# Graph network kernel: convolutions that read a 16-bit copy of the edge counts, with features in three 16-bit parts

## What is computed

```python
def gcn_conv(x, W, b, src, dst, n_nodes):
    ones = jnp.ones(src.shape[0], dtype=x.dtype)
    deg = jax.ops.segment_sum(ones, dst, num_segments=n_nodes)
    dinv = jnp.where(deg > 0, jax.lax.rsqrt(deg), 0.0)
    norm = dinv[src] * dinv[dst]
    h = x @ W
    msg = h[src] * norm[:, None]
    out = jax.ops.segment_sum(msg, dst, num_segments=n_nodes)
    return out + b
...
h = gcn_conv(x, W1, b1, src, dst, n)
h = jax.nn.relu(h)
h = gcn_conv(h, W2, b2, src, dst, n)
return jax.nn.log_softmax(h, axis=1)
```

## Time and profile before

| | us |
|---|---|
| median of 3 runs | 3497.33 (3475.69 to 3510.03) |
| the profiled execution | 3489.9 |
| its span, first to last instruction | 3488.1 |
| PE busy, of the span | 2740.4 (79%) |
| DVE busy | 2218.7 (64%) |
| ACT busy | 1601.9 (46%) |
| DMA, mean over the span | 117 GB/s |

### The profile page before, as it was taken

How to read it: one execution, slowest core, us unless ns; L and a number is a source line. 1 busy time by engine, 2 the same in 40 slices (tenths; PEclk the granted TensorE clock), 3 DMA queues, 4 the chain that set the end, 5 groups by cost and what they waited for, 6 DMA issues and landing times. The chain is left out here.

```text
span 3488.1 us, 63284 instructions
## 1 busy us (share of the span) xinstructions
PE 2740.4 (79%) x21694; PEld 2254.5 (65%) x21694; DVE 2218.7 (64%) x4911; ACT 1601.9 (46%) x2729; POOL 201.0 (6%) x481
## 2 busy tenths in 40 slices
PE   2887777524354888798883999979998999979998
PEld 1555554402043666576662898969897899968997
DVE  8999998300046999799995555555555555545555
ACT  1555554200023888688883444434444444434443
POOL 1000000000000000000000111001110111001110
PEclk9999999767657999889996999999999999989999
DMA  2666666795805333532320333223331233223331
GB/s 56 149 148 148 148 149 163 166 238 143 196 2 160 113 113 113 157 113 102 111 91 9 133 112 127 94 78 112 126 110 71 103 125 110 94 76 118 121 112 54
DMA packets 164745, 406.93 MB, mean 117 GB/s; under 512 B 123705, under 2 KB 135793, under 8 KB 136048
## 3 DMA queue, kind: packets, MB, share of 16 engines
q1 hardware_dynamic: 164573, 404.67, 39.7%
HBM read 322.84 MB, written 80.77 MB: 116 GB/s over the span
## 5 line engine op out<-in xcount | busy, mean ns | idle before, releaser
L1604 DVE CUSTOM_DVE_ANT_0 l_arow<-l_scores,abias 125x500 f32<-125x500 f32 (+1 forms) x525 | 325.5, 622 | 368.6 <-issue 314.7
L1540 PE MATMUL l_asum<-vals,l_awcol 125*125 125x129 f32 x3750 | 516.2, 277 | 34.6 <-DVE l_awcol L934 34.3
L1540 PEld LDWEIGHTS l_asum<-vals,l_awcol 125*125 125x125 f32 x3750 | 454.6, 187 | 61.9 <-DVE l_awcol L934 52.9
L1193 PE MATMUL gturned<-ident,grow 125*125 125x125 f32 x2500 | 410.3, 306 | 30.0 <-ACT grow L1133 30.0
L1193 PEld LDWEIGHTS gturned<-ident,grow 125*125 125x125 f32 x2500 | 333.0, 204 | 108.0 <-issue 73.2
L1102 DVE SCALAR_TENSOR_TENSOR grow<-line,a_dst 125x3125 f32<-125x3125 f32 x100 | 347.6, 3476 | 52.4 <-DMA line<-lines_dram 44.1
L1575 ACT ACTIVATE l_arow<-l_arow,l_aneg 125x500 f32<-125x500 f32 (+1 forms) x525 | 323.5, 659 | 81.1 <-DVE l_aneg L1610 81.1
L932 ACT ACTIVATE l_awcol<-l_aturned 125x500 f32<-125x500 f32 (+1 forms) x225 | 122.8, 546 | 516.2 <-PE l_aturned L1549 516.2
L1133 ACT ACTIVATE grow<-grow,neg 125x3125 f32<-125x3125 f32 x100 | 290.4, 2904 | 137.3 <-DVE neg L1114 137.3
L1111 DVE CUSTOM_DVE_ANT_0 grow<-grow,bias 125x3125 f32<-125x3125 f32 x100 | 341.7, 3417 | 16.8 <-DMA bias<-bias_dram 1.8
L1171 PE MATMUL gparts<-gwcol,h_mem 125*32 125x125 f32 x5000 | 244.5, 291 | 122.2 <-ACT gwcol L1146 122.2
(11 more groups left out here) (300 smaller groups left out, 4464.4 us busy)
## 6 DMA issues: line engine op xcount, KB each, us to landing
abias<-bias_dram SPq DMA_DIRECT2D x100, 1562.5 KB, 6.5
bias<-bias_dram SPq DMA_DIRECT2D x50, 1562.5 KB, 6.5
counts<-counts_dram SPq DMA_DIRECT2D x41, 1367.2 KB
bias_dram<-lnrow SPq DMA_DIRECT2D x25, 1562.5 KB, 6.8
counts_dram<-blk SPq DMA_DIRECT2D x25, 1367.2 KB
line<-lines_dram SPq DMA_DIRECT2D x8, 1367.2 KB
counts<-counts_dram SPq DMA_DIRECT2D x41, 158.7 KB
fixed<-kp SPq DMA_DIRECT2D x250, 4.0 KB, 2.5
```

Source lines behind the costliest of these rows:

```text
L1193: last = pe.transpose(bank[q % RING][:, j // 4, j % 4 * T:(j % 4 + 1) * T], row[n % RING][:, t * T:(t + 1) * T], ident[0:T, 0:T])
L1540: last = pe.matmul(sum_ps[p][:, :], wcol[c % T_BANKS][:, j * T:(j + 1) * T], vals[:, t, :], start=(t == 0), stop=(t == NT - 1))
L1604: dve.tensor_tensor_reduce(out=row[p][:, a:z], in0=s_ps[c % S_BANKS][:, 0:z - a], in1=bias[p][0:T, a:z], scale=1.0, scalar=-3.0e38, op0=AL ...
```

## The change

The counts are also written as bf16, to a second array `counts16_dram` (0.78 MB a tile). In `build_counts` ACT casts five rows of `blk` in each slot (125 casts of 125 x 625 elements), and SP writes two blocks of destinations at a time (runs of 500 bytes, as before), in slot 2 of every odd block from b = 3 on, eleven times while blocks are still being made, once in the last step and once, for the single last block (runs of 250 bytes), after the last `bias_home`. The fp32 counts are still written.

In the convolution stage, `u` is split by DVE into three bf16 parts (`in_pieces`), which stand side by side in 48 of 64 columns (`u_pieces`). PE takes the tiles in pairs on 64 columns each, thirteen groups a round, in bf16. Fourteen tiles are loaded in the first block, 20 are held. Counts over 256 are not exact in bf16, so a loop after the fourth group of each round reads whole fp32 tiles into `agg`, takes off the rounded part, and adds the product of the rest in fp32. It runs once where no degree is over 256, and 25 times otherwise; the trip count comes from the largest degree, found in the first block (`most`, `trips`). ACT's copies of the sums now start chunk by chunk (`sum_ready`), and so does PE's turn.

```diff
+        blk16 = [sb(f"blk16_{p}", [T, NT, 2 * T], BF16) for p in range(2)]
...
+                def counts16_home(q):
+                    blocks = range(2 * q, min(2 * q + 2, NT))
+                    sp.wait_ge(cast_done, SLOTS * (blocks[-1] + 1))
+                    a, z = blocks[0] * T, (blocks[-1] + 1) * T
+                    load_rows(sp, G["counts16_dram"][:, :, a:z].rearrange("t s d -> s t d"), blk16[q % 2][:, :, 0:z - a], counts16_out[q % 2])
...
                         counts_home(b - 1)
                     if k == 1 and b >= 2:
                         bias_home(b - 2)
+                    if k == 2 and b >= 3 and b % 2 == 1:
+                        counts16_home((b - 3) // 2)
                 bias_home(NT - 1)
+                counts16_home(NT // 2)
...
+                            act.wait_ge(cast_done, SLOTS * (b - 1))
                             act.wait_ge(counts_out[b % 2], LANDED * (b // 2))
...
+                        q, half = g // 2, g % 2
+                        if k == 0:
+                            act.wait_ge(win_read, 2 * SLOTS * b)
+                            if half == 0 and q >= 2:
+                                act.wait_ge(counts16_out[q % 2], LANDED * (q // 2))
+                        part = slice(NT // SLOTS * k, NT // SLOTS * (k + 1))
+                        act.activation(blk16[q % 2][:, part, half * T:(half + 1) * T], blk[g % 2][:, part, :], ACT.Copy).then_inc(cast_done, 1)
...
-    SLOTS, EARLY = 9, 6
+    EARLY, LATE, PIECES, WIDE_U = 14, 2, 3, 64
+    SLOTS = (EARLY + 4 + LATE) // 2
+    EXACT = 256
...
-        for r, order in enumerate((range(NT), [*range(NT - SLOTS, NT), *range(NT - SLOTS)])):
-            for i, t in enumerate(order):
-                if i % 4 == 0:
-                    groups.append([])
-                if t not in held:
+        for order in (range(len(pairs)), [*range(len(pairs) - SLOTS, len(pairs)), *range(len(pairs) - SLOTS)]):
+            for i in order:
+                if i not in held:
                     slot = len(loads) if len(loads) < SLOTS else held.pop(next(iter(held)))
-                    loads.append((t, slot, last_use[slot]))
-                    held[t] = slot
-                last_use[held[t]] = len(groups)
-                groups[-1].append((t, held[t], sum(1 for _, k, _ in loads if k == held[t])))
+                    loads.append((i, slot, last_use[slot]))
+                    held[i] = slot
+                groups.append((i, held[i], sum(LANDED * len(pairs[k]) for k, there, _ in loads if there == held[i])))
+                last_use[held[i]] = len(groups)
+        final = [[max(g for g, (i, _, _) in enumerate(groups) if g // half_groups == r and len(pairs[i]) > j) for j in range(2)] for r in range(2)]
+        def load(sp, n):
+            i, slot, after = loads[n]
             if after:
                 sp.wait_ge(group_used, after)
-            load_rows(sp, counts[slot][:, :], G["counts_dram"][t, :, :], counts_in[slot])
+            for j, t in enumerate(pairs[i]):
+                load_rows(sp, counts[2 * slot + j], G["counts16_dram"][t, :, :], counts_in[slot])
+        def in_pieces(dve, m, rest):
+            piece = lambda k: u_pieces[:, :, k * HID:(k + 1) * HID]
+            chain(dve, m, dve.tensor_copy(piece(0), u[:, :, :]))
+            chain(dve, m, dve.tensor_tensor(rest, u[:, :, :], piece(0), ALU.subtract))
+            chain(dve, m, dve.tensor_copy(piece(1), rest))
+            chain(dve, m, dve.tensor_tensor(rest, rest, piece(1), ALU.subtract))
+            return dve.tensor_copy(piece(2), rest)
...
+                    dve.tensor_reduce(most[:, :], deg, AX.X, ALU.max).then_inc(most_ready, 1)
+                    chain(dve, m, dve.tensor_tensor(pick[:, :], ident[:, 0:HID], ident[:, HID:2 * HID], ALU.add))
+                    for j in (2 * HID, WIDE_U, WIDE_U + HID, WIDE_U + 2 * HID):
                         chain(dve, m, dve.tensor_tensor(pick[:, :], pick[:, :], ident[:, j:j + HID], ALU.add))
                     chain(dve, m, dve.tensor_scalar(G["has_in"][:, :], deg, 0.0, None, ALU.is_gt))
                     dve.tensor_scalar(G["dinv"][:, :], deg, 1.0, None, ALU.add).then_inc(deg_ready, 1)
+                    bank = banks.full(dve, "most", 0)
+                    dve.tensor_reduce(most[0:1, :], bank[0:1, 0:T], AX.X, ALU.max).then_inc(banks.read["dve"], 1)
+                    banks.done(dve, "most")
+                    chain(dve, m, dve.tensor_scalar(most[0:1, :], most[0:1, :], float(EXACT), float(NT - 1), ALU.is_gt, ALU.mult))
+                    chain(dve, m, dve.tensor_scalar(most[0:1, :], most[0:1, :], 1.0, None, ALU.add))
+                    dve.tensor_copy(trips[:, :], most[0:1, :])
...
+                    banks.done(dve, "u")
+                    in_pieces(dve, m, conv[:, :, :])
...
+            whole = agg[0:T, 0:N]
+            rounded = convs.enter_context(nc.sbuf_tensor("rounded", [T, N], BF16))
+            half = NT * D // 2
+            for memory in (G["h_mem"][:, 0:NT * D], work[:, :, :].rearrange("p t d -> p (t d)")):
+                both = memory.bitcast(BF16)
+                counts += [both[:, 2 * half * p:2 * half * p + N] for p in range(2)]
+            counts += [convs.enter_context(nc.sbuf_tensor(f"late{p}", [T, N], BF16))[:, :] for p in range(LATE)]
+            REST_AT = 3
-                    for i in range(EARLY, len(loads)):
+                    n, turns = sp.alloc_register("rest_trips"), sp.alloc_register("rest_turns")
+                    sp.reg_mov(turns, 1)
+                    sp.reg_load(n, trips[0:1, 0:1])
+                    def whole_counts():
+                        with sp.Fori(0, sp.snap(n, min_val=1, max_val=NT)) as j:
+                            sp.wait_ge(rest_used, sp.snap(turns, min_val=1, max_val=2 ** 24))
+                            load_rows(sp, whole, G["counts_dram"][bass.ds(j, 1), :, :].rearrange("a s d -> s (a d)"), whole_in)
+                            sp.reg_add(turns, turns, 1)
+                    for i in range(EARLY // 2, SLOTS):
                         load(sp, i)
+                    whole_counts()
+                    for i in range(SLOTS, len(loads)):
+                        load(sp, i)
+                    whole_counts()
...
+                    pe.sem_inc(rest_used, 1)
...
+                        pair, slot, landed = members
+                        pe.wait_ge(counts_in[slot], landed)
                         for c, (a, z) in enumerate(CHUNKS):
-                            for j, (t, slot, _) in enumerate(members):
-                                done = pe.matmul(sum_ps[c][32 * j:32 * j + 32, 0:z - a], u_wide[:, t, :], counts[slot][:, a:z],
-                                                 start=(i == 0), stop=(i == half_groups - (1 if j == 0 else 2)))
-                        done.then_inc(group_used, 1)
+                            for j, t in enumerate(pairs[pair]):
+                                done = pe.matmul(sum_ps[c][WIDE_U * j:WIDE_U * (j + 1), 0:z - a], u_pieces[:, t, :], counts[2 * slot + j][:, a:z],
+                                                 start=(i == 0), stop=(g == final[r][j]))
+                            if i == half_groups - 1:
+                                done.then_inc(sum_ready, 1)
+                            elif c == NC - 1:
+                                done.then_inc(group_used, 1)
                         if i == half_groups - 1:
-                            pe.wait_ge(sum_copied, NC * (r + 1))
-                            for t in range(NT):
-                                last = pe.matmul(rows_ps[:, t * HID:(t + 1) * HID], vcols[:, t * T:(t + 1) * T], pick[:, :],
-                                                 start=True, stop=True)
+                            pe.sem_inc(group_used, 1)
+                        if i == REST_AT:
+                            with pe.Fori(0, pe.snap(n, min_val=1, max_val=NT)) as _:
+                                pe.wait_ge(rest_made, pe.snap(turns, min_val=1, max_val=2 ** 24))
+                                for c, (a, z) in enumerate(CHUNKS):
+                                    done = pe.matmul(sum_ps[c][0:HID, 0:z - a], u_one[:, :], whole[:, a:z], start=False, stop=False)
+                                done.then_inc(rest_used, 1)
+                                pe.reg_add(turns, turns, 1)
+                        if i == half_groups - 1:
+                            for c in range(NC):
+                                pe.wait_ge(sum_copied, NC * r + c + 1)
+                                for t in tiles_of(c):
+                                    last = pe.matmul(rows_ps[:, t * HID:(t + 1) * HID], vcols[:, t * T:(t + 1) * T], pick[:, :],
+                                                     start=True, stop=True)
...
-                        act.wait_ge(group_used, half_groups * (r + 1))
...
+                            act.wait_ge(sum_ready, NC * r + c + 1)
...
+                    def rest():
```

(12 more changed lines are left out.)

43 lines of the change are left out of this document (28 added, 15 removed).

## The result

The changed kernel takes 3394.7 us (median of 4 runs, 3386.6 to 3399.2), the kernel before 3492.6 beside it: a ratio of 0.972, with an interval of 0.966 to 0.977. The forecast was 3400. The profiled execution took 3386.6, its span is 3384.8.

What follows compares the result with a forecast made beforehand. DVE was taken to bound `build_counts`, and reading counts the convolution stage. The span 3488.1 - 143 (convolution) + 38 (second write) + 13 (tail) + 2 (casts) = 3398, plus 2 around it: 3400 us, range 3370 to 3430.

Steps and rivals of the forecast that it cites:

- What bounds each round of the convolution stage: Convolution stage: whole fp32 tile last in SP's list, there at 29.3 us, then DVE 5.7 and products 8; stage -143.
- The groups and the turn behind the rest: Convolution stage, each round: nine groups of 1.8 us, 16.2 together, then a turn of 9.3 with no wait.
- my bounds of -157 to -123: Convolution stage: groups 1.3 and products 5.4 us at full clock give -157; groups 2.6 and products 10.8 give -123.
- Weight loads (rival): Convolution stage: PE's weight loads no longer hide, 0.9 us a group, 23 over 26 groups, total 3423 or 3443; chance 0.18.
- The casts: `build_counts`: 125 casts on ACT at 0.75 us each cost nothing in ACT's idle time, +2 in the tail.
- The second write: `build_counts`: 16-bit write delays the slot-3 fetch, DVE waits 3.5 us, eleven times, +38; bounds 0 and 101.
- The tail: End of `build_counts`: twelfth 16-bit write and single block delay the next stage, +13, between +11 and +16.
- The rival that the queue costs more in `build_counts`: `build_counts`: the whole 9.2 us of each write reach DVE, +101 instead of +38, total 3463; chance 0.11.
- The rival that the fetches are in time: `build_counts`: 16-bit data overlap the bias write or DVE is late itself, the 38 vanishes, total 3362; chance 0.18.

## Why the prediction was right, and where it was not

The median was 5 us off and the span 13. The mechanisms that the forecast named are those that acted, but larger misses of both signs lie in the sum, and that they nearly cancel is luck.

- **What bounds each round of the convolution stage: right.** The whole tile was there 29.7 us after the first product (forecast 29.3), DVE took 5.3 (5.7), the products 7.2 (8). With the tile first, the stage fell to 92.3: the cause is shown.
- **The groups and the turn behind the rest: mis-sized.** I took 1.8 us from fp32 groups in a stage with a mean clock of 0.66, and 9.3 for a turn from the same rows. But mean clock over a stage with long waits is not the clock of nine groups in a row. The windows around the products, the nine groups and the turn:

```profile
785.30:792.40 7.10, 7.10 (x14) 1.50 (x14) 0.00 (x0) 0.00 (x0) 0.00 (x0) 0.75 0.91 229
792.40:804.60 12.20, 12.20 (x121) 7.06 (x120) 0.00 (x0) 1.10 (x3) 0.00 (x0) 1.00 0.08 20
804.50:810.70 6.20, 6.20 (x51) 6.11 (x50) 0.00 (x0) 2.15 (x6) 0.00 (x0) 0.89 0.00 0
```

  The clock rose during the products (0.75 to 1.00), and a group took 1.33 us; the turn took 6.2. That is 4 and 3 us a round: rounds of 60.4 and 62.0 for 68.5 and 70.3, and the stage 128.3 where 144 of my 147.5 were for it. Error: -16. With the 2.6 ahead of the stage this part came to -160, outside my bounds of -157 to -123: they let the groups and products follow the clock and left the turn at 9.3. The turn follows it too; in the second profile of the same kernel the first one took 8.5 us at 0.64 and the second 6.0 at 0.92.
- **Weight loads (rival): fell.** In the second window 120 loads take 7.06 us within 12.20 in which products are always busy; 1.33 us is 3125 columns at 2.4 GHz (1.30) and no more. The Trainium skill ("TensorE: Matmul & The Clock Gate", Part 3, The mechanism) has loads overlap products in flight only where the row group differs, though it also has a load into the background weight buffer pulled ahead; here all loads were for the same rows and yet hidden, so against the "only" the measurement decides.
- **The casts: right.** ACT's groups in `build_counts` (count, then busy us, mean ns):

```profile
L542 ACT ACTIVATE blk<-win 125x325 f32<-125x325 f32 x248 | 95.7, 441 | 232.7 <-PE win L497 232.7
...
L563 ACT ACTIVATE blk<-blk 125x625 bf16<-125x625 f32 x119 | 89.4, 752 | 0.0
```

  0.752 us each (0.75), and ACT still waits for PE.
- **The second write: cause right, size by luck.** Forecast eleven waits of 3.5, +38; measured +31.6, of it 29.9 in eleven waits of 2.7, at the place that was forecast. The working held: I had the list issued 4.3 us before DVE wants it (394 and 398.29) and landing 7.8 after its issue; over the eleven blocks the means are 4.9 and 7.6, where before they were 10.3 and 3.1. But the 3.5 was worked out from a trace with 47 ns a packet. On the chip with 48 (the whole fp32 tile first, same `build_counts`) the means are 5.6 and 6.3, only eight of the eleven lists are late, and they cost 9.3 us. Without register reads, which otherwise make DVE come later, it is 22.4 us at 48 ns, 2.0 each. The term that was mis-sized is the 3.5; that +31.6 is near 38 goes with a chip of 52 ns.
- **Register reads: not foreseen.** +18.3 us of DVE idle time ahead of `hot_key`. The row of before showed 7.1 us in 12 gaps, and I hadn't read it. With the waits for fetches it makes 50 of the 53.5 us. The two are not independent: with the reads gone, 12 of 23 us were gained.
- **The tail: right, near its upper end.** +15.5 (13, with bounds 11 and 16, and 2 more for the casts): the single block's 250-byte runs held SP for 11.4 us, no less than 500-byte runs do (9.1 just ahead of them), and a 250-byte packet took 50.8 ns on average where a 500-byte one took 52.5, so runs count, not bytes.
- **The rival that the queue costs more in `build_counts`** fell as it was put: the whole 9.2 us did not reach DVE. More was lost all the same, +69 with the tail where I had 51 to 53, through the register reads.
- **The rival that the fetches are in time** fell here, and held for three of the eleven lists on the chip with 48 ns.

The span was forecast at 3398 and is 3384.8. The errors: -16 in the convolution stage, -1 ahead of it, -13 behind it (within the spread of the profiles), +18 for the reads, -6 for the fetches, +4 for what else `build_counts` gained, and +0.5 in the tail with the 2 us of the casts counted in.

## What to carry to other kernels

A transfer that must pass before anything else can go on belongs at the head of its list: one 1.56 MB tile at the end of SP's list cost 41 us in two rounds, at the front 3. A write of many short runs is priced by its runs and by what it delays, not by its bytes; when it must be, give the small transfers behind it two slots more of lead (the stage ended 18 us earlier on one chip, 49 on another, and not at all where the queue was not full), and keep it off the tail. A second queue is no cure if it puts two such writes side by side. And read the "issue" rows of the engine that sets the pace: a gap with no wait in the profile can grow with the load on the queue.

## What the runs showed of the hardware

- A register read on DVE, hidden between operations in most slots, left gaps of up to 1.1 us while 500-byte runs were being written: 25.4 us over a stage, 0 with the reads gone. Why is open.
- The same 500-byte packets took 47 to 48 ns on two chips and 52 on a third. The kernel before did not notice; the changed one lost 25 us more in `build_counts` on the chip with 52, and nothing more with six buffers.
- A write of GpSimd's in a queue of its own, beside a count write in SP's, stretched that from 10 to 20 us from issue to last packet, and a 4 KB fetch behind it took up to 15.9 us to land. DVE's waits came to 64.8 us, against 14 to 36 with one queue and the same four buffers.
- SP's issue of the 13-row part of a write of short runs took 3.7 to 6.9 us in the stage (median 4.1 to 4.6), and 7 to 12 where such writes followed one another.
- 250-byte packets took as long as 500-byte ones: 43 to 57 ns against 47 to 53, means of a run.
- PE's turn of 50 records took 5.6 to 6.2 us at a granted clock of 0.89 to 0.99, and 10.7 at 0.50.
